# New orders for all engines in a transformer tower over images on one core: each group of images gets its own places in the order tables

## What is computed

```python
pooled = x.reshape(B, 12, 14, 16, 14, 16).sum(axis=(3, 5))
h = einsum('bcij,ce->bije', pooled, channel_weights).reshape(B, 196, 192)
q, k, v = split(layernorm(h) @ W_qkv + b_qkv)
h = h + softmax(q @ k.T / sqrt(192)) @ v
W0 = w_fc * C0; b0 = b_fc * c0b          # C0, C1: masks mixed by alpha_e and alpha_r
W1 = w_proj * C1; b1 = b_proj * c1b
h = h + gelu(layernorm(h) @ W0.T + b0) @ W1.T + b1      # hidden width 768
```

## Time and profile before

| | |
|---|---|
| time, median of 3 runs | 488.52 us (488.26 to 488.54) |
| the profiled execution, time and span | 490.17 us, 488.4 us |
| busy: PE, DVE, ACT, POOL | 427.2, 380.4, 287.0, 255.6 us |
| mean granted clock of PE | 0.918 |
| read from HBM, written | 156.29 MB, 9.63 MB |
| instructions | 10,938 |

### The profile page before, as it was taken

How to read it: one execution, slowest core, us unless ns; L and a number is a source line. 1 busy time by engine, 2 the same in 40 slices (tenths; PEclk the granted TensorE clock), 3 DMA queues, 4 the chain that set the end, 5 groups by cost and what they waited for, 6 DMA issues and landing times.

```text
span 488.4 us, 10938 instructions
## 1 busy us (share of the span) xinstructions
PE 427.2 (87%) x4558; PEld 363.8 (74%) x4558; DVE 380.4 (78%) x272; ACT 287.0 (59%) x478; POOL 255.6 (52%) x194
## 2 busy tenths in 40 slices
PE   5976266986999999989998989899999989999996
PEld 4543144874678889878887878788888878888996
DVE  1688999989899999798989898989999888610000
ACT  1022035623859685849584939586868656877821
POOL 1022314703647582747475838465756575576840
PEclk9999555995599999989999989999999989999999
DMA  8999999999999999999999999999999996001101
GB/s 239 324 405 406 406 406 405 406 408 409 407 404 408 409 407 409 406 402 407 406 410 405 410 407 406 408 402 409 410 409 410 403 407 264 28 26 39 37 26 51
DMA packets 56661, 166.65 MB, mean 341 GB/s; under 512 B 5972, under 2 KB 13030, under 8 KB 56612
## 3 DMA queue, kind: packets, MB, share of 16 engines
q1 hardware_dynamic: 56612, 165.95, 87.2%
HBM read 156.29 MB, written 9.63 MB: 340 GB/s over the span
## 4 chain that ended last, share of the span: by engine, by line
DMA 46%; DVE 23%; PE 18%; SPq 7%; issue 4%; ACT 0%; DVEq 0%
DMA xs<-x 46%; DVE pooled L476 21%; PE ps L604 18%; SPq L408 6%; DVE phat_tok L494 1%; DVE prod L485 0%; ACT out_sb L1018 0%; SPq L425 0%; PE ps L801 0%; DVE var L490 0%; PE ps L781 0%; DVE u_tok L504 0%; PE ps L788 0%; SPq L448 0%; DVE row_inv L502 0%
## 5 line engine op out<-in xcount | busy, mean ns | idle before, releaser
L476 DVE TENSOR_REDUCE pooled<-xs 128x28 f32<-128x1792 f32 x144 | 328.9, 2323 | 28.8 <-DMA xs<-x 28.5
L1116 POOL TENSOR_TENSOR h_lo<-h_f,h_hi 128x784 fp32r<-128x784 f32 x96 | 177.2, 1870 | 74.9 <-ACT h_hi L1012 74.7
L604 PE MATMUL ps<-w_hi,h_hi 128*98 128x192 f32 x768 | 207.7, 270 | 0.5 <-POOL h_lo L1116 0.5
L604 PE MATMUL ps<-w_lo,h_hi 128*98 128x192 f32 x768 | 197.1, 257 | 0.0
L604 PE MATMUL ps<-w_hi,h_lo 128*98 128x192 f32 x768 | 196.7, 256 | 0.0
L604 PEld LDWEIGHTS ps<-w_hi,h_hi 128*98 128x98 f32 x768 | 129.0, 168 | 15.6 <-issue 14.2
L604 PEld LDWEIGHTS ps<-w_lo,h_hi 128*98 128x98 f32 x768 | 129.5, 169 | 0.0
L604 PEld LDWEIGHTS ps<-w_hi,h_lo 128*98 128x98 f32 x768 | 129.2, 168 | 0.0
L1003 ACT ACTIVATE h_f<-ps 128x784 f32<-128x784 f32 x96 | 75.8, 826 | 21.0 <-PE ps L604 20.1
L1012 ACT CAST h_hi<-h_f 128x784 fp32r<-128x784 f32 x96 | 78.4, 856 | 0.0
L1093 POOL TENSOR_TENSOR inv<-var,minus_half 98x8 f32<-98x8 f32 x16 | 26.2, 1639 | 75.9 <-DVE var L490 75.7
(11 more groups left out here) (119 smaller groups left out, 344.9 us busy)
## 6 DMA issues: line engine op xcount, KB each, us to landing
xs<-x SPq DMA_DIRECT2D x336, 448.0 KB, 12.2
out<-out_sb SPq DMA_DIRECT2D x32, 294.0 KB
rows_sb<-wfc SPq DMA_DIRECT2D x1, 576.0 KB, 5.6
out_sb<-wproj SPq DMA_DIRECT2D x1, 576.0 KB, 11.1
h_f<-wqkv SPq DMA_DIRECT2D x1, 432.0 KB
cf<-const_full SPq DMA_DIRECT2D x1, 264.0 KB, 3.1
h_f<-const_paired SPq DMA_DIRECT2D x1, 153.0 KB, 3.5
cr<-const_rows SPq DMA_DIRECT2D x1, 83.2 KB
```

The source lines that it names most:

```text
L476: dve.tensor_reduce(pooled[:, n % 2, t, GRID * first:GRID * end].rearrange("p (i j) -> p i j", j=GRID), runs, AX.XY, ALU.add).then_inc(red ...
L604: return pe.matmul(o, a, b, start=start, stop=stop, skip_group_check=shared)
L1116: pool.tensor_tensor(h_lo[:, m % 2, t], h_f32[:, t], h_hi[:, m % 2, t].bitcast(F32), ALU.subtract).then_inc(h_lo_ready, 1)
```

## The change

All entries of the five tables are new, but for some of the first groups; the units, their instructions and their semaphores stay as they are. Groups 1 to 5 now have entries that differ from the pattern of the groups after them; before, these were groups 1 to 4. Of the diff, the rows that the prediction speaks of (the entries are of groups 0 to 15, in this order; in `project`, rows 2, 4, 5, 8, 10, 11, 12 and 18 to 22 of 24, old then new; in `reduce`, rows 5 to 8 of 9):

```diff
-STEPS = 4907
+STEPS = 4905
...
-    "sum_rows": (443, 399, 379, 379, 370, 383, 371, 360, 348, 336, 325, 312, 318, 310, 312, 330),
...
-    "scores": (545, 624, 528, 543, 506, 528, 514, 502, 490, 479, 467, 455, 443, 422, 451, 430),
-    "turn_maxima": (601, 693, 643, 596, 573, 579, 568, 556, 544, 533, 520, 498, 497, 488, 485, 464),
-    "turned_scores": (615, 707, 657, 610, 588, 595, 583, 571, 560, 548, 536, 513, 512, 503, 513, 480),
-    "weigh": (644, 739, 695, 646, 619, 631, 619, 608, 596, 584, 572, 544, 543, 549, 559, 516),
-    "turn_context": (663, 780, 732, 675, 643, 658, 646, 634, 623, 611, 598, 587, 570, 572, 590, 542),
...
+    "sum_rows": (443, 396, 379, 392, 372, 366, 356, 340, 333, 326, 318, 311, 316, 302, 293, 285),
...
+    "scores": (545, 624, 520, 491, 525, 506, 533, 547, 540, 533, 526, 485, 487, 458, 419, 403),
+    "turn_maxima": (581, 662, 585, 591, 567, 566, 600, 593, 585, 578, 571, 525, 521, 492, 468, 437),
+    "turned_scores": (595, 676, 598, 606, 581, 580, 614, 606, 599, 592, 585, 539, 547, 508, 483, 452),
+    "weigh": (624, 706, 637, 663, 611, 625, 654, 646, 639, 632, 625, 585, 581, 538, 514, 509),
+    "turn_context": (642, 727, 681, 691, 643, 651, 686, 679, 671, 664, 659, 608, 605, 571, 537, 535),
...
     "residual": (
-        (720, 836, 1053, 1046, 1031, 1019, 1007, 996, 984, 972, 960, 960, 928, 924, 893, 828),
-        (970, 1174, 1187, 1157, 1145, 1134, 1122, 1110, 1098, 1086, 1080, 1065, 1032, 1042, 997, 913),
+        (700, 827, 976, 1023, 1011, 999, 992, 985, 978, 964, 961, 946, 939, 920, 876, 812),
+        (972, 1090, 1143, 1144, 1113, 1106, 1099, 1091, 1084, 1102, 1069, 1070, 1053, 1035, 981, 897),
     ),
...
     "hidden": (
-        (778, 940, 909, 882, 894, 882, 870, 859, 847, 835, 817, 805, 793, 798, 778, 670),
...
+        (778, 882, 891, 880, 870, 898, 891, 884, 877, 869, 830, 844, 807, 782, 737, 653),
...
     "project": (
...
-        (931, 1127, 1116, 1097, 1100, 1088, 1077, 1051, 1038, 1035, 1029, 1020, 1000, 1002, 964, 875),
...
-        (899, 1073, 1111, 1092, 1080, 1069, 1057, 1045, 1033, 1030, 1009, 1006, 976, 997, 949, 864),
-        (937, 1138, 1153, 1117, 1105, 1094, 1082, 1070, 1058, 1046, 1035, 1031, 1005, 1013, 970, 886),
...
-        (942, 1143, 1158, 1123, 1111, 1099, 1087, 1076, 1063, 1060, 1040, 1036, 1011, 1007, 975, 881),
...
-        (905, 1068, 1091, 1077, 1065, 1053, 1042, 1030, 1017, 1010, 994, 991, 953, 977, 938, 848),
-        (952, 1149, 1164, 1128, 1116, 1105, 1093, 1081, 1069, 1066, 1045, 1042, 1016, 1018, 981, 897),
-        (1012, 1208, 1221, 1168, 1156, 1144, 1133, 1121, 1109, 1097, 1089, 1082, 1042, 1081, 1017, 933),
...
-        (1023, 1217, 1235, 1246, 1234, 1223, 1216, 1205, 1192, 1175, 1173, 1143, 1076, 1113, 1050, 949),
-        (1051, 1185, 1202, 1173, 1162, 1150, 1138, 1126, 1114, 1102, 1095, 1097, 1081, 1063, 1006, 944),
-        (1061, 1222, 1246, 1252, 1240, 1228, 1222, 1210, 1198, 1186, 1179, 1153, 1087, 1118, 1055, 955),
-        (1018, 1247, 1241, 1199, 1187, 1175, 1164, 1152, 1140, 1128, 1131, 1113, 1047, 1058, 1033, 976),
-        (1056, 1283, 1197, 1228, 1216, 1204, 1196, 1184, 1172, 1160, 1157, 1129, 1062, 1087, 1044, 928),
...
+        (939, 1058, 1098, 1097, 1050, 1064, 1057, 1050, 1043, 1056, 1033, 1025, 1005, 986, 948, 832),
...
+        (899, 1036, 1028, 1043, 1075, 1050, 1043, 1036, 1028, 1022, 1015, 1005, 980, 980, 922, 837),
+        (949, 1063, 1108, 1107, 1080, 1070, 1063, 1055, 1048, 1062, 1038, 1030, 1011, 1006, 959, 864),
...
+        (944, 1069, 1103, 1102, 1086, 1075, 1068, 1061, 1054, 1067, 1044, 1035, 1016, 1000, 953, 875),
...
+        (910, 1041, 1047, 1063, 1091, 1084, 1077, 1070, 1062, 1027, 1021, 1010, 986, 955, 927, 843),
+        (955, 1074, 1114, 1113, 1097, 1089, 1082, 1075, 1068, 1073, 1049, 1041, 1030, 1011, 964, 880),
+        (1013, 1189, 1222, 1161, 1170, 1163, 1156, 1152, 1141, 1144, 1120, 1115, 1090, 1065, 1001, 933),
...
+        (1023, 1103, 1179, 1181, 1207, 1200, 1192, 1185, 1178, 1166, 1162, 1159, 1145, 1085, 1012, 928),
+        (983, 1154, 1164, 1166, 1212, 1205, 1198, 1191, 1183, 1184, 1168, 1164, 1140, 1070, 1039, 906),
+        (1054, 1160, 1195, 1239, 1218, 1210, 1203, 1196, 1189, 1189, 1173, 1170, 1151, 1102, 1044, 960),
+        (988, 1109, 1159, 1199, 1131, 1123, 1116, 1109, 1102, 1111, 1079, 1081, 1109, 1107, 1022, 911),
+        (1059, 1123, 1213, 1219, 1136, 1129, 1122, 1114, 1107, 1119, 1084, 1086, 1065, 1056, 1017, 949),
...
 DVE_ORDER = {
...
-        (313, 277, 269, 247, 243, 234, 233, 216, 207, 198, 189, 192, 190, 191, 200, 228),
-        (342, 307, 298, 276, 273, 271, 262, 253, 244, 235, 226, 221, 238, 239, 230, 257),
-        (363, 345, 318, 320, 300, 309, 282, 291, 282, 273, 264, 259, 258, 259, 250, 277),
-        (387, 365, 338, 347, 338, 329, 320, 311, 302, 293, 285, 279, 278, 279, 280, 297),
...
+        (313, 277, 269, 252, 243, 234, 225, 216, 207, 198, 189, 181, 172, 166, 168, 164),
+        (342, 325, 298, 289, 280, 271, 262, 253, 237, 228, 219, 210, 201, 203, 198, 212),
+        (363, 345, 318, 327, 318, 309, 300, 273, 264, 255, 239, 230, 229, 223, 236, 232),
+        (387, 365, 338, 347, 338, 329, 320, 293, 285, 276, 267, 258, 267, 265, 256, 252),
...
-    "maxima": (581, 662, 556, 574, 545, 556, 527, 518, 509, 501, 495, 474, 475, 436, 464, 443),
...
+    "maxima": (561, 642, 563, 554, 545, 536, 577, 568, 559, 550, 541, 503, 501, 472, 448, 416),
...
 POOL_ORDER = {
-    "scale_p": (493, 442, 433, 424, 415, 441, 444, 432, 421, 371, 362, 356, 367, 341, 368, 370),
...
+    "scale_p": (493, 422, 427, 432, 415, 430, 397, 389, 380, 371, 362, 382, 398, 342, 338, 315),
...
     "low_part": (
-        (818, 986, 949, 921, 934, 922, 910, 901, 892, 887, 857, 872, 839, 841, 818, 709),
-        (836, 1005, 967, 972, 975, 963, 951, 920, 911, 905, 898, 890, 857, 860, 837, 728),
...
+        (818, 922, 946, 919, 928, 941, 934, 927, 920, 913, 869, 884, 868, 846, 790, 693),
+        (836, 963, 964, 960, 947, 960, 953, 945, 938, 931, 888, 902, 887, 864, 808, 712),
...
 SP_ORDER = {
     "load": (
...
-        (330, 332, 321, 307, 298, 289, 280, 265, 256, 248, 244, 239, 235, 234, 235, 243),
...
+        (344, 346, 335, 321, 312, 303, 299, 285, 276, 267, 258, 249, 235, 226, 229, 225),
...
     "send": (
-        (1066, 1272, 1285, 1255, 1244, 1231, 1220, 1208, 1196, 1180, 1176, 1163, 1130, 1140, 1095, 1011),
-        (1188, 1405, 1398, 1379, 1367, 1355, 1343, 1332, 1319, 1308, 1312, 1276, 1275, 1243, 1180, 1096),
+        (1084, 1202, 1255, 1256, 1225, 1218, 1211, 1203, 1196, 1213, 1178, 1182, 1160, 1144, 1093, 1009),
+        (1193, 1342, 1386, 1377, 1365, 1359, 1351, 1344, 1327, 1327, 1312, 1305, 1286, 1241, 1178, 1094),
```

More of the change, by code:

```diff
@@ L70 @@
 PERIOD = 254
-STEPS = 4907
+STEPS = 4905
 PE_ORDER = {
-    "sum_rows": (443, 399, 379, 379, 370, 383, 371, 360, 348, 336, 325, 312, 318, 310, 312, 330),
-    "turn_phat": (518, 475, 471, 450, 443, 470, 471, 459, 448, 421, 410, 397, 395, 366, 396, 397),
-    "apply_a": (531, 487, 494, 473, 466, 495, 495, 483, 472, 444, 432, 420, 419, 400, 414, 410),
-    "scores": (545, 624, 528, 543, 506, 528, 514, 502, 490, 479, 467, 455, 443, 422, 451, 430),
-    "turn_maxima": (601, 693, 643, 596, 573, 579, 568, 556, 544, 533, 520, 498, 497, 488, 485, 464),
-    "turned_scores": (615, 707, 657, 610, 588, 595, 583, 571, 560, 548, 536, 513, 512, 503, 513, 480),
-    "weigh": (644, 739, 695, 646, 619, 631, 619, 608, 596, 584, 572, 544, 543, 549, 559, 516),
-    "turn_context": (663, 780, 732, 675, 643, 658, 646, 634, 623, 611, 598, 587, 570, 572, 590, 542),
-    "turn_u": (701, 813, 753, 706, 671, 707, 695, 684, 672, 660, 648, 636, 592, 626, 607, 570),
-    "apply_g2": (714, 826, 788, 735, 699, 728, 717, 705, 693, 682, 669, 658, 610, 641, 632, 589),
+    "sum_rows": (443, 396, 379, 392, 372, 366, 356, 340, 333, 326, 318, 311, 316, 302, 293, 285),
+    "turn_phat": (518, 454, 461, 457, 445, 457, 424, 419, 412, 405, 387, 413, 433, 379, 368, 343),
+    "apply_a": (531, 467, 500, 471, 501, 486, 511, 531, 524, 517, 510, 451, 448, 431, 392, 362),
+    "scores": (545, 624, 520, 491, 525, 506, 533, 547, 540, 533, 526, 485, 487, 458, 419, 403),
[3 more added lines that the diff above has]
+    "turn_context": (642, 727, 681, 691, 643, 651, 686, 679, 671, 664, 659, 608, 605, 571, 537, 535),
+    "turn_u": (681, 751, 741, 731, 693, 687, 724, 717, 710, 703, 686, 672, 636, 598, 553, 553),
+    "apply_g2": (694, 765, 772, 751, 730, 727, 754, 747, 739, 732, 719, 695, 650, 618, 588, 573),
@@ L120 @@
 ACT_ORDER = {
[L121 to L132 removed]
[6 rows of a table removed]
+    "load_exp": (360, 618, 449, 488, 502, 486, 509, 525, 518, 511, 504, 500, 459, 464, 429, 390),
+    "copy_p_tok": (455, 406, 396, 412, 395, 379, 368, 350, 343, 336, 328, 321, 337, 320, 306, 303),
+    "copy_phat": (525, 462, 468, 466, 494, 478, 506, 522, 515, 508, 501, 440, 443, 420, 381, 355),
+    "copy_b": (540, 477, 513, 485, 517, 501, 524, 541, 534, 526, 519, 467, 474, 452, 413, 382),
```

(22 more changed lines are left out.)

13 lines of the change are left out of this document (1 added, 12 removed), and 94 rows, old and new, of tables (ACT_ORDER, DVE_ORDER, PE_ORDER, POOL_ORDER).

## The result

| kernel | median | lowest to highest | runs | ratio, 95% interval |
|---|---|---|---|---|
| before | 487.44 us | 486.20 to 490.64 | 20 | |
| changed | 489.82 us | 488.91 to 491.31 | 20 | 1.0036, 1.0021 to 1.0051 |
| changed, once more beside other runs of before | 489.63 us against 487.78 | 488.96 to 490.63 | 12 | 1.0033, 1.0017 to 1.0050 |

What follows compares the result with a forecast made beforehand. The end was taken as the moment the last late data reach PE plus the PE work queued behind. Of two tail places, +2.2 and +1.2 us, the later end counts: +2.2 on the median 488.52 gives 490.7 us, range 487.4 to 494.0.

Steps and rivals of the forecast that it cites:

- the first place: turn_maxima(13) on PE: can't start before 388.6 us, with 7.0 us of work added behind it; end 487.0, +2.2 us.
- rival 1: Half clock doesn't come back after the new PE wait: first place gives +0.5 us, time 489.0 us; chance 0.27.
- Loads: Image loads on the DMA queues don't move: the last load lands at 414.9 us in both kernels.
- rival 3: Image stream has room, loads freed earlier land earlier: -2.9 to -11.3 us, near end 485.6 us; chance 0.12.
- Front: Groups 0 to 5: group 1's first hidden unit comes 5.8 us earlier; costed at nothing, as PE later waits for images anyway.
- Tail, second place: sum_rows(15) on PE: starts at 418.3 us, 2.8 us earlier data but 4.0 us more work behind it; end 485.9, +1.2 us.
- Middle: Groups 6 to 11: at most 11.3 us of PE waits to win; costed at nothing, if PE comes no more than 3 us later.
- theory B: Experiments' theory, one queue: several places met in turn, each bound by images just landed, so repairing one leaves the next.
- A: Experiments' theory, the middle: PE loses it in groups 6 to 12, at sum_rows and turn_maxima; the tail meets a late PE.
- rival 2: POOL becomes the bound, scale_p(15) ahead of two low parts, which end at 437.0: one late +4.1 us, 492.6 us; chance 0.13.

Runs made afterwards that it cites:

- the yardstick: Profile of the kernel with groups 0 to 5 in the new order and the rest old; its profiled execution took 486.46 us.
- the mixed kernel: Old kernel with groups 0 to 5 taking the new entries, 6 to 15 the old ones: 487.43 us, 0.9995 to the kernel before.
- changed, maxima earlier: Changed kernel with DVE's maxima of groups 6 to 10 and 13 one reduction earlier: 490.60 us, 1.0054 to the kernel before.
- changed, middle later: Changed kernel with PE's sum_rows(m+1) and turn_maxima(m), m = 6 to 10, behind residual(m-2,1) and two project units: 489.95 us, 1.0037 to the kernel before.
- the last experiment: Old kernel with sum_rows(15) alone moved ahead of hidden(13,0), weigh(14) and four project units: 494.74 us against 487.44, 1.0146.

## Why the prediction was right, and where it was not

**The sum was right, and its making only in part.** +2.2 was forecast and +2.4 measured. The forecast let the first place decide and the second come in under it. The runs show no single place that decides. PE's last wait for images is at a place between the two that the forecast did not cost, turn_maxima(14), and the limits that the two places set lie about half a microsecond or less below it.

**That the number came out is in part luck.** Where the stream ended at 414.9 in both, PE ended at 484.73 before and at 485.13 in the changed kernel: +0.4 us, about the +0.5 that rival 1 has from the first place, and its condition (no half clock behind the wait) held. The rest of the 2.1 us found below is the 1.7 us by which that profile of before is itself worse than the yardstick (69.8 against 68.1 in the table below); about as much is what its stretch of half clock cost. The forecast kept that stretch on both sides, and so it came to +2.2 from a profile that lies 2.7 us above the median of its kernel. The measured 489.82 us lies between rival 1's 489.0 and the forecast's 490.7, about as far from either.

**Loads.** The DMA engines were as full as forecast (1.03, 406 GB/s), and no slice of 12 us on any run's page moved more than 414. The landing isn't the fixed 414.9 that the step took: the changed kernel landed its last load at 413.6 and at 414.9, the old order at 412.9 (the yardstick), 414.6 and 414.9. So rival 3 fell, but a bound of "within 1 us" was too tight. The Trainium skill's ceiling of 435 GB/s (DMA: Bandwidth & Descriptors, Where 436 GB/s comes from) isn't reached in any of these slices.

**Front.** Costed at nothing; the mixed kernel measured 0.9995.

**Tail, first place.** Its arithmetic for the start was exact where the stream ended as before: turn_maxima(13) at 388.6 forecast, 388.53 measured. The wait was 1.27 and 1.79 us, not some 3, since PE itself came later. The half clock kept in the sum didn't return, as rival 1 had it. In the profile that ended its stream at 414.9, PE ends 485.13 - 388.53 = 96.6 us behind turn_maxima(13); the forecast had 487.0 - 388.6 = 98.4. The difference of 1.8 us is about that term of 1.7, with a wait of 0.38 us at turn_maxima(14) in the 96.6 that the sum had not. And with turn_maxima(13) two units later, its wait moved to sum_rows(14) and the end stayed. So taking away the first place's wait alone gave nothing that these runs can measure.

**Between the two places.** The new order of DVE, reduce(15,5) ahead of maxima(14), was counted for what it does to sum_rows(15), and its other side was not: turn_maxima(14) now waits for that reduce. In both profiles of the changed kernel the chain runs through it, and PE ends 78.7 us behind the landing of that load (483.88 - 405.17 and 485.13 - 406.44). In the old order maxima(14) came first, and the yardstick's PE has no wait for pooled or phat_tok behind 365.95.

**Tail, second place.** Sum_rows(15) was forecast at 418.3 and started at 418.53 where the stream ended at 414.9. By the landing of the last load:

| | sum_rows(15) behind the landing | PE's end behind sum_rows(15) | end behind the landing |
|---|---|---|---|
| old order, the yardstick | 417.38 - 412.9 = 4.5 | 481.02 - 417.38 = 63.6 | 68.1 |
| old order, the profile before | 6.2 | 63.6 | 69.8 |
| old order, again | 421.50 - 414.6 = 6.9 | 63.6 | 70.5 |
| changed | 417.27 - 413.6 = 3.7 | 66.6 | 70.3 |
| changed, again | 418.53 - 414.9 = 3.6 | 66.6 | 70.2 |
| changed, turn_maxima(13) later | 417.38 - 413.7 = 3.7 | 66.6 | 70.2 |
| changed, maxima earlier | 418.58 - 414.3 = 4.3 | 66.6 | 70.9 |
| changed, middle later | 418.43 - 415.0 = 3.4 | 66.6 | 70.0 |

Against the yardstick, sum_rows(15) of the changed kernel's two profiles comes 0.8 to 0.9 us earlier behind the landing and has 3.0 us more behind it: +2.1 us, with medians 1.85 and 2.38 us apart. The other two profiles of the old order had stretches of half clock, 3.4 and 6.8 us long. The columns split the end and do not by themselves show what sets it: in the changed kernel sum_rows(15) starts 0.4 us later than its data would let it (417.27 against 416.68 + 0.15). Had PE been on time there, the end would have been 69.8 us behind the landing (an estimate from these rows), so the move of sum_rows(15) accounts for some 1.7 of the 2.1 as a limit, and PE's wait at turn_maxima(14) for the rest. No run took away the wait at turn_maxima(14) alone; it could give back 0.4 us at most. The term was +1.2 in the forecast, for two reasons. The 2.8 us by which sum_rows(15) was to come earlier were taken from a run in which it stood 6.2 us behind the landing, 1.7 more than in the yardstick; and the 4.0 us of work came out as 3.0 (0.4 of it is a wait of PE for rows_sb that the yardstick has there and the changed kernel has not; the rest I can't name). The last experiment takes the place apart: the earlier sum_rows(15) on PE alone costs 4 us and the half clock behind it. That the new order of DVE, reduce(15,5) ahead of maxima(14), pays part of that back is argued from the rows and not shown: no run changed DVE's order there alone.

**Middle.** Costed at nothing on the ground that the tail is met whatever PE did before. The waits changed their names and not their sum (12.7 us from 200 to 400 in the yardstick, 13.9 in the changed kernel). Two other orders of the middle, with the waits at other places and none at turn_maxima(14), brought no gain. That fits the step and theory B, but the seven units moved ahead of sum_rows(15) fit A and B alike: PE has no idle time there. Whether a middle without those waits, together with the old tail, would give the 2 us back is open; no run here had one.

**POOL (rival 2).** Scale_p(15) did come ahead of the low parts, which ended at 427.57 + 7.31 = 434.9 and not 437.0, and PE has no wait for h_lo behind 393.4. POOL in order of time, against the earlier trace rows:

```profile
419.54 1.64 POOL L1093 TENSOR_TENSOR inv<-var,minus_half 98x8 f32<-98x8 f32 x1 [6.93 <-DVE var L490]
...
421.73 3.69 POOL L1116 TENSOR_TENSOR h_lo<-h_f,h_hi 128x784 fp32r<-128x784 f32 x2
...
427.57 7.31 POOL L1116 TENSOR_TENSOR h_lo<-h_f,h_hi 128x784 fp32r<-128x784 f32 x4
```

## What to carry to other kernels

Where a stream sets the pace, find the last place at which the late engine waits for a piece of it, and count the work behind that place, for every unit that hangs on late data and not only for the last. Moving the consumer of the last data forward in its queue gains only what it had waited, and pays for all the work that it overtakes: in the last experiment 4.1 us. A wait that is moved away from one unit showed up at its neighbour, since both hang on the same late data, and here three parts of an order that was laid out as a whole cost more than all of it. Before a profile is taken as the base of a sum, see where its own time lies among the runs.

## What the runs showed of the hardware that was not expected

The stream's end moved between two executions of the changed kernel by 1.3 us (413.6 and 414.9), at the same bytes and a queue as full; over the eight profiles of the table above it lay between 412.9 and 415.0. No run shows why.

The half clock fell in different places from one execution to the next, and not by the length of the wait before it alone. A stretch of 3.4 us at 0.50 came just behind waits of PE of 1.80 us, 2.0 and 4.04 us, and none behind one of 1.79. In the run of the last experiment none came behind one of 2.87 us either; the granted clock was 1.00 from there to 300 us:

```profile
283.79 0.39 PE L801 MATMUL ps<-cf,uhat_tok 98*128 98x98 f32 x2 [2.87 <-POOL uhat_tok L1109]
```

The old kernel run again had a stretch of 6.8 us in the middle of the stream, 0.85 us behind a wait of 2.25 us at sum_rows(13), with PE busy all through it; that execution took 490.65 us, where the median of its runs was 487.06. The wait and the stretch:

```profile
367.75 0.73 PE L604 MATMUL ps<-sel_gram,pooled 128*98 128x96 f32 x6 [2.25 <-DVE pooled L476]
```

```profile
368.60:375.40 6.80, 6.80 (x46) 5.60 (x45) 5.90 (x7) 3.23 (x6) 4.79 (x5) 0.50 1.03 398
```
